# Grouped attention: the first step of the running maximum reads key tiles 0 and 1 from SBUF

## The reference

```
qn  = layernorm(x);  q = qn @ Wq / 8;  k, v = split(media @ Wkv)      # 16 heads of 64
sim = q k^T;  sim = where(media_mask, sim, -3e38)                      # 1601 keys
attn = softmax(sim);  x = x + tanh(attn_gate) * ((attn @ v) @ Wo)
x   = x + tanh(ff_gate) * gelu(layernorm(x) @ W1) @ W2
```

## Time and profile before

| | |
|---|---|
| unprofiled executions | 5325.75, 5329.64, 5330.6 us |
| the profiled execution | 5337.48 us, its span 5335.6 us |
| granted TensorE clock, mean | 0.946 |
| PE busy | 4767.3 us (89%) |
| DVE busy | 3858.5 us (72%) |
| ACT busy | 3191.6 us (60%) |
| POOL busy | 2611.4 us (49%) |

### The profile page before, as it was taken

One profiled execution on the slowest core, in us unless ns is written; L12 is line 12 of the kernel. 1 busy time (PEld: TensorE's weight loads), 2 busy tenths in 40 slices (PEclk: granted clock), 3 DMA queues, 4 the chain that ended last, 5 costly groups with the idle time before them and its releaser, 6 DMA issues. The chain is left out here.

```text
span 5335.6 us, 91911 instructions
## 1 busy us (share of the span) xinstructions
PE 4767.3 (89%) x29848; PEld 3532.8 (66%) x29848; DVE 3858.5 (72%) x5212; ACT 3191.6 (60%) x4815; POOL 2611.4 (49%) x1723
## 2 busy tenths in 40 slices
PE   6999999999977998798999969875999999999987
PEld 5777777777746776465555649654777777777766
DVE  5998898889864443576666746335888898898874
ACT  5777777777752555355555520235777777777762
POOL 3777777777750332111111132001777777777761
PEclk9999999999988999799999979887999999999998
DMA  1000000000000000222222200111000000000000
GB/s 53 7 1 8 7 7 1 7 8 1 1 16 26 0 0 0 51 44 41 40 46 42 32 34 0 56 53 36 1 7 8 8 1 8 8 1 8 1 1 32
DMA packets 35078, 93.96 MB, mean 18 GB/s; under 512 B 12896, under 2 KB 22368, under 8 KB 33504
## 3 DMA queue, kind: packets, MB, share of 16 engines
q1 hardware_dynamic: 34656, 88.47, 7.4%
HBM read 55.80 MB, written 2.10 MB: 11 GB/s over the span
## 5 line engine op out<-in xcount | busy, mean ns | idle before, releaser
L736 POOL TENSOR_TENSOR L_attn_sums<-L_attn_sums,L_attn_probs 128x1024 f32<-128x1024 f32 x512 | 1227.1, 2397 | 103.8 <-POOL L_attn_sums L736 80.7
L1010 ACT ACTIVATE L_attn_probs<-L_attn_ps_s,L_attn_bias_now 128x512 f32<-128x512 f32 x1664 | 1105.6, 688 | 125.3 <-PE L_attn_ps_s L773 100.1
L914 DVE TENSOR_TENSOR L_attn_ps_x<-L_attn_probs,L_attn_ps_x 128x512 f32<-128x512 f32 x1408 | 978.9, 695 | 142.7 <-ACT L_attn_probs L1010 97.6
L926 DVE TENSOR_TENSOR L_attn_probs<-L_attn_probs,L_attn_ps_x 128x3072 f32<-128x3072 f32 (+2 forms) x384 | 933.6, 2459 | 86.0 <-PE L_attn_ps_x L822 86.0
L1016 ACT ACTIVATE L_attn_probs<-L_attn_probs 128x3072 f32<-128x3072 f32 (+2 forms) x384 | 775.0, 2051 | 140.2 <-DVE L_attn_probs L926 136.7
L809 PE MATMUL L_attn_ps_u<-L_attn_probs,L_attn_v_sb 128*64 128x256 f32 (+1 forms) x6656 | 777.1, 384 | 0.0
L771 PE MATMUL L_attn_ps_s<-L_attn_g_hi,L_attn_ctx_hi 128*128 128x512 f32 x1664 | 713.3, 429 | 55.1 <-issue 34.3
L1536 ACT ACTIVATE L_cross_probsT<-L_cross_ps_st 128x512 f32<-128x512 f32 (+1 forms) x832 | 490.8, 597 | 374.3 <-PE L_cross_ps_st L1280 355.7
L1418 DVE TENSOR_REDUCE L_cross_part<-L_cross_ps_s 128x1 f32<-128x804 f32 x512 | 498.1, 992 | 246.7 <-PE L_cross_ps_s L1267 242.9
L773 PE MATMUL L_attn_ps_s<-L_attn_g_hi,L_attn_ctx_lo 128*128 128x512 f32 x1664 | 668.6, 402 | 0.0
L772 PE MATMUL L_attn_ps_s<-L_attn_g_lo,L_attn_ctx_hi 128*128 128x512 f32 x1664 | 667.7, 401 | 0.0
(11 more groups left out here) (285 smaller groups left out, 9013.9 us busy)
## 6 DMA issues: line engine op xcount, KB each, us to landing
L_cross_kx<-A SPq DMA_DIRECT2D x256, 100.5 KB, 2.8
L_attn_ctx_in<-in_ctxT SPq DMA_DIRECT2D x16, 804.0 KB, 4.4
memory_ctx<-in_ctx SPq DMA_DIRECT2D x8, 832.0 KB, 5.9
Bw<-in_ctxT SPq DMA_DIRECT2D x8, 804.0 KB, 5.3
memory_ctxT<-in_ctxT SPq DMA_DIRECT2D x8, 804.0 KB, 4.4
A<-in_L_mlp_w SPq DMA_DIRECT2D x4, 1024.0 KB, 6.0
X<-in_x SPq DMA_DIRECT2D x1, 2048.0 KB, 8.5
L_norm_wq<-in_L_w_wq SPq DMA_DIRECT2D x2, 1024.0 KB, 7.9
```

Source lines behind the costliest of these rows:

```text
L736: pool.tensor_tensor(both, both, p[:, k:k + 2, :], ALU.add).then_inc(added_up, 1)
L914: dve.tensor_tensor(high[:, :] if k == KT - 1 else ps_x[:, :], tile, ps_x[:, :], ALU.max).then_inc(maxed, 1)
L926: dve.tensor_tensor(s, s, ps_x[:, :].unsqueeze(1).to_broadcast([P, count, W]), ALU.subtract).then_inc(shifted, 1)
L1010: act.activation(probs[j % 2][:, k, :], ps_s[(KT * j + k) % 4][:, :], ACT.Identity, bias=bias_now[:, k:k + 1]).then_inc(taken, 1)
```

## The change

The running maximum starts with tile 1 in place of tile 0. Its first step takes the maximum of tiles 1 and 0, both read from SBUF, and writes it to `ps_x`; the copy of tile 0 into `ps_x` is gone. A slot has 12 steps in place of 13, and the values of `maxed` follow.

```diff
@@ turn_tops(J), TensorE
-                pe.wait_ge(maxed, KT * (J + 1))
+                pe.wait_ge(maxed, (KT - 1) * (J + 1))
@@ running_max(J, j, k), VectorE
-                if k == 0:
-                    dve.tensor_copy(ps_x[:, :], tile).then_inc(maxed, 1)
+                if k == 1:
+                    dve.tensor_tensor(ps_x[:, :], tile, probs[j % 2][:, 0, :], ALU.max).then_inc(maxed, 1)
                 else:
-                    dve.wait_ge(maxed, KT * J + k)
+                    dve.wait_ge(maxed, (KT - 1) * J + k - 1)
                     dve.tensor_tensor(high[:, :] if k == KT - 1 else ps_x[:, :], tile, ps_x[:, :], ALU.max).then_inc(maxed, 1)
@@ slot(b, j, first, last), VectorE
-                for k in range(KT):
+                for k in range(1, KT):
                     running_max(J, j, k)
```

## The result

| | median, us | executions | against before |
|---|---|---|---|
| before, same chip | 5327.69 | 4 (5325.28 to 5330.60) | |
| changed | 5379.31 | 4 (5370.71 to 5395.27) | 1.0095 [1.0068, 1.0122] |

The change makes the kernel slower, as forecast, but by 51.6 us here, where the prediction said 18; the time lies outside its range.

The account below looks back on a forecast made before the run. TensorE's wait for `high`, the running maximum's last step (41.4 us), was taken as what counts. Terms 0 + 1 + 13.3 + 3.8 = 18 us on 5329.6 gave 5347.7, stated as 5347.5 us; range 5332 to 5358.

Parts of the forecast that it names:

- the register operation: VectorE, between two waits: 40 ns paid once a slot at the last wait, 84 x 0.045 = 3.8 us, bounds 0 and 8.4.
- The copy is worth nothing: Start of each slot: removing 88.2 us of VectorE copies saves 0, being ahead of the last wait for ScalarE.
- GpSimd stops the new first step: VectorE's L911, two SBUF inputs: blocked until GpSimd's instruction is nearly through; median near 1.12 us, near 1.8 in j = 7.
- The rule of the Trainium skill: VectorE instructions with two SBUF inputs contend with GpSimd instructions reading SBUF; whoever comes second is blocked until the first is done.
- The fixed cost by source: PSUM sources cost 120 cycles, SBUF 58, making the new step about 0.06 us shorter; left out of the sum.
- The rival "no stop": GpSimd does not stop the new step: 5334 us, or 5330 with the register operation hidden; no stop or hidden cost 0.18.
- j = 7: Slots j = 7: last maximum 0.73 us late, then L934 and L742 change order; 14 x 0.95 = 13.3 us.
- Slots 3 and 5: Slots j = 3 and 5, 32 in all: the stopped first step loses 0.01 to 0.03 us each, 1 us.
- What is outside of the attention is fixed: The sum has no term for other phases; TensorE's wait for L930 and its 3.44 us pause were taken as fixed.
- The rival "TensorE's clock": Longer TensorE idle at j = 7 draws another low-clock stretch: 14 x 1.7 = 24 us more, 5372 us; chance 0.08.
- The faster rival: The copy was on the path, so TensorE's 41.4 us wait for `high` goes: 5288 us; chance 0.05.

Follow-up runs that it names:

- the step alone: Changed kernel whose first step (two SBUF inputs) counts 2 on the semaphore, so no second register operation is needed: 5346.79 us, 1.0035 of the kernel before.
- 8.4 alone: Kernel before, its copy kept but counting on its own semaphore, so the changed kernel's wait values and register operation are needed: 5340.53 us, 1.0010 of before.
- the kernels with short additions: Kernel before and changed kernel, GpSimd's additions cut from 512 to 16 columns except in each phase's first two slots: 5297.48 us (0.9940) and 5317.50 us (0.9990).

## Why the prediction was wrong

The direction held, and so did the mechanism inside of the attention phases; the size did not. Two steps failed. The larger: nothing outside of the attention has a term in the sum, and no reason is given for that; in the four executions of the result 29 of the 51.6 us are not the attention's. The smaller: the register operation was priced at 3.8 us and cost 8.8. Against its own steps:

- *The copy is worth nothing:* right. The wait before tile 9 in slot 20 is still 0.63 us with the copy gone, and no phase gained. TensorE's wait for `high` grew, it did not shrink.
- *GpSimd stops the new first step:* right. Forecast 1.12 us at the median and near 1.8 at j = 7; measured 1.106 and 1.81, beginning 0.14 us before GpSimd's end; without GpSimd's additions 0.71. The rule of the Trainium skill ("SBUF — State Buffer", Who interferes with whom) held, for an output in PSUM too, which the earlier trace rows could not show. The fixed cost by source of the Trainium skill ("VectorE: DVE Perf Modes", The TRN2 errata) doesn't show here: undisturbed the new step takes 700 ns, an old one 695. The rival "no stop" is refuted.
- *j = 7:* right in each turn (L736, then L742, L934, L937, L710) and nearly in size: 13.3 forecast; with the step alone 10.1 us at j = 7 and, by the start of L829, 2.5 more behind it, 12.6. In slot 31 the end of L937 lies 5.24 us behind the start of `high`, 5.03 before: with 0.73 that is 0.94, against the 0.95 taken. Slots 3 and 5: 1 us forecast, 0.5 measured.
- *The register operation:* here the sum failed first. Taken 3.8 us, "40 ns, once a slot"; measured 8.4 alone, 12.0 between the kernels with short additions, 8.8 (22.2 - 13.4) as the rest of the changed kernel's first profile. The term was mis-sized because I priced the operation by its own 40 ns. What counts is how much later the step behind it starts, and that is 0.08 us. It also brought the breaks of 0.3 us, 3.6 us in all; the trace before has one, of 0.3 us. The upper bound of 0.1 a slot covered the one, not the others. With 8.8 the sum would have been 23, and the attention's 21.0 to 24.9 in six profiles would have been met.
- *What is outside of the attention is fixed:* here the range failed. By the attention alone the changed kernel is 22 us slower, and that is just where its lower group lies (5353.3 against 5331), inside of the range. The remaining 7 to 29 us of the three medians come from the upper group, at a lower granted clock. The one profile of the upper group has the lost time in the self-attention of layer 1, where the clock falls a second time for 51.2 us; the windows of before show this phase as one that begins just as the clock comes back (0.63 from 1680 to 1730 us, 0.96 in the 50 us behind). I did not look outside the changed phases. And the three times of before, within 5 us, told nothing of an upper group that has 4 in 62 of its executions.
- *The rival "TensorE's clock":* it had the right engine, and nearly the right time (5372) by luck, for it had another place and trigger: j = 7 of the attention, "from the point where an idle time of about 1 us lowers the clock". TensorE's idle time there did grow (its wait at L829 in slot 31 is 1.12 us, 0.91 before), and the low stretch between the last `high` of a batch and the next one did grow by 3.4 us in six of 14 places; in two it is gone, which leaves 13.7 us more in all. The j = 0 slots got 4.3 us longer by this and by L829's later start (2.6), where the rival had 24. (It also took the pause of 3.44 us for one of all 14 places; one of over 3 us stands at 10 of them, the passes of the loop after its first.)

The faster rival, 5288 us, was refuted by the first point. The best of the kernels that compute the reference is the one before with its bias copied first, 5308.3 us, 0.9953 [0.9935, 0.9971].

## What to carry to other kernels

An instruction that saves work off the path can still cost: look at what each operand shares with the other engines, above all in the stage that has the least reserve before its last wait. Price an operation of the sequencer between two waits by how much later the next instruction starts, and if new values can be had without one (here by counting 2 on the first step, 8.8 us of 22), take them. And when a change is valued in one phase, look in the windows for other phases in which the clock has just risen, time the kernel before often enough to see its slower executions, and widen the range by what one more stretch at the lower level costs there (here 21.9 us).

## What the runs showed of the hardware that was not expected

- A register operation of 40 ns between two waits of VectorE made the step behind it 0.077 to 0.080 us later.
- With it came breaks of VectorE's instruction stream of 0.3 us, with all data ready, at a fixed instruction of the loop's pass. Their cause was not tested.
- A copy of 128x13 that takes 0.17 us took 1.25, 1.03 or 0.58 us, by which instruction of GpSimd it met; exchanging it with its neighbour brought 20.6 us in one kernel and 2.5 in the other.
- TensorE's granted clock fell a second time, 13.6 us after it had risen and with TensorE 49.2 of 51.2 us busy from then on, in one profile of six of the same code, at a price of 21.9 us. By their mean clock, 11 of 22 executions of that kernel and 4 of 62 of the one before may have had something of the kind. What decides it is open; a phase reached 9.5 us later had 1 of 12.
- From the last `high` of a batch to the next one the clock is at the 1.2 GHz level for 0, 3.4 or 6.8 us. In the changed kernel's first profile the six slots with 3.4 us more of it got 0.34 to 1.75 us longer, the two with 3.4 us less 1.35 and 1.43 shorter.
